# Attention phases of a two-layer kernel: a batch's value matmuls and finish steps at other places in the order

## The chip, the cores and the metric

The kernel runs on one core of one Trainium2 chip. The metric is device time in microseconds of one execution; lower is better. Three executions of the kernel before took 381.69, 383.87 and 384.30 us, median 383.87.

## The reference

The reference is two layers over 4 batches of 256 tokens of width 256: a retention block, a mixture of 8 experts, an attention block with 32 query heads over 8 key groups (head size 8), and a gated feed-forward block with 2:4 sparsity. Each block adds tanh(gate) times its result to x. The change lies in the attention block, which computes:

```
q = (Q @ w_q.T).reshape(B, S, G, HG, HD);  k, v likewise per group
scores = einsum('bnghd,bmgd->bnghm', q, k) / sqrt(HD)     # padded keys and later keys masked
attn = softmax(scores, axis=-1)
out = einsum('bnghm,bmgd->bnghd', attn, v).reshape(B, S, D) @ w_o.T + b_o
```

## The kernel before, in words

All engines have their programs written out by hand; each runs its instructions in order and waits on counted semaphores. The helper `acquire` (line 185) hands out the eight PSUM banks in rotation by kind and makes TensorE wait until the bank's last content has been read. The kind "max" has three banks (0 to 2), "exp" three (3 to 5), "turn1" and "tok1" one each (6 and 7).

The attention block runs as one phase for each of the four batches, and a phase has 24 steps (line 552 for TensorE, line 956 for ScalarE, line 1284 for VectorE). In step n of phase b the work is this.

- **Scores of the next batch** (`scores`, line 414): one matmul of 512 columns and one mask matmul into a "max" bank, four steps ahead (`LEAD`; seven ahead in phase 0). VectorE reads each bank with one maximum over keys (`row_maxima`, line 1213). After the 24th, `negate` (1218) makes the negated maxima, and `neg_turn` (432) turns them on TensorE in two transposes through the one "turn1" bank; ScalarE copies each to `nmT`, and the sync engine's queue moves them by two DMAs into `qst`. The first `weights` of the next phase waits for these DMAs through the semaphore `max_rows` (line 444).
- **Weights of this batch** (`weights`, line 439): one matmul of 512 columns into an "exp" bank. ScalarE makes the exponentials of it (line 929), and GpSimd zeroes the diagonal blocks (line 775) after exponentials 4, 8, 10 and 12 of each half.
- **Values of this batch** (`values`, line 448): four groups of 32-column matmuls, called v0 to v3 here: half 0 and half 1 of the groups, each for the first and the second 128 queries. v0 and v2 have 8 matmuls, v1 and v3 have 16. v0 and v1 are read by VectorE (`value_copy`, 1232), v2 and v3 by ScalarE (`value_turn`, 932). v0 and v1 stand at steps 20 and 22 (`VALUES_AT`). v2 and v3 stand after step 23, v2 in an "exp" bank and v3 in "tok1", each followed by two of the four leading scores of batch b+2.
- **Finish of the batch before** (`finish`, lines 462, 939, 1239): twelve steps, six for each 128 queries. Four transpose the values through "turn1" and VectorE divides by the sum (a reciprocal and a product). The fifth transposes the result through "turn1", and ScalarE copies it. The sixth projects it into "tok1", and VectorE adds it to x and makes its statistics. They stand at the odd steps 1, 3, ... 23.
- **Queries and keys of batch b+2** (phases 0 and 1 alone): two layer-norm transposes through "turn1" at steps 10 and 12, the query projection at 14, half the keys at 13 and two stack pieces at 19 and 21. After step 23 come the other half of the keys and two more stack pieces.

Phase 3 has neither scores nor queries; in their place it has four layer-norm transposes for the feed-forward block at steps 13, 15, 17 and 19.

Of the kernel before, what the change touches and what calls it, by code (L numbers as in the profile page):

```python
# [33 lines left out]

NORM_STEPS, LATE_NORM_STEPS = (13, 15, 17, 19), (3, 4, 6, 7)
KEYS_AT, STACK_AT = 13, (19, 21)
VALUES_AT = (20, 22)
NEGATE_AT, FIRST_NEGATE_AT = 22, 18
LN_EPS, GN_EPS = 1e-5, 1e-3
MASKED = -float(2.0 ** 100)  # L40
# [3 lines left out]
def build_program(nc, a, out):  # L44
# [6 lines left out]
    with ctx:  # L51
# [5 lines left out]
        def sem(name):  # L57
            if name not in sems:
                sems[name] = ctx.enter_context(nc.semaphore(name))
            return sems[name]  # L60
# [136 lines left out]
        def filled(eng, stage, i):  # L197

            eng.wait_ge(sem(stage + "_ready"), i + 1)
            return fills[stage, i]  # L200
# [4 lines left out]
        def taken(ins, stage):  # L205
            ins.then_inc(sem(stage + "_taken"), 1)
# [32 lines left out]
        def _(pe):  # L239
# [174 lines left out]
            def scores(b, n):  # L414

                s = b % 2
                q, hg, nt, quads = score_fill(n)
                if n % 12 == 0:
                    pe.wait_ge(sem(f"ks{q}_taken"), b + 1)
                    stage, i = stack_fill(b, 2 * q + 1)  # L420
                    pe.wait_ge(sem(stage + "_taken"), i + 1)
                if n == 0:
                    if b == 0:
                        loaded(pe, "caus", 2)
                dst = acquire(pe, "sa", 24 * b + n, "max").rearrange("p (j m) -> p j m", m=(nt + 1) * P)
                pe.matmul(dst, qst[:, s, q, hg, tile_cols(nt)], kblk[s][q][:, quads, 0:(nt + 1) * P],  # L426
                          start=True, stop=False, skip_group_check=True)
                diagonal = dst[:, :, nt * P:(nt + 1) * P]
                ready(pe.matmul(diagonal, identb[:, :], causb[:, 0:diagonal.shape[1], :], start=False, stop=True,  # L429
                                skip_group_check=True), "sa")  # L430
# [17 lines left out]
            def values(b, i, kind):  # L448

                q, nt = divmod(i, 2)  # L450
                stage = VALUE_STAGES[q]
                pe.wait_ge(sem("causal_done"), 8 * b + 4 * q + 2 + 2 * nt)
                dst = acquire(pe, stage, 2 * b + nt, kind)
                pe.wait_ge(sem("vp_taken"), b + 1)
                for mt in range(nt + 1):
                    for j in range(QUADS):
                        rhs = pt0[q][:, j, :, tile_cols(nt)] if mt == 0 else pt1[q][:, j, :, :]
                        ins = pe.matmul(dst[32 * j:32 * j + 32, :], vaug[:, 2 * b + mt, 4 * q + j, :], rhs,  # L458
                                        start=(mt == 0), stop=(mt == nt), skip_group_check=True)
                ready(ins, stage)  # L460

            def finish(b, n):

                nt, c = divmod(n, 6)
                i = 2 * b + nt
                if c < PER_GROUP:
                    f = 4 * i + c
                    dst = acquire(pe, "avT", f, "turn1")
                    if c == 0:
                        for stage in VALUE_STAGES:  # L470
                            pe.wait_ge(sem(stage + "_taken"), i + 1)
                    for q in range(HALVES):
                        ins = pe.transpose(dst[:, tile_cols(q)], avT[nt][:, q, c * P:(c + 1) * P], ident[:, :])  # L473
                    ready(ins, "avT")
                elif c == PER_GROUP:
                    pe.wait_ge(sem("avT_taken"), 4 * i + 4)
                    turn_pair("atT", i, att[:, i % 2, :], "turn1")
                else:
                    dst = acquire(pe, "res2", i, "tok1")[:, 0:DIM]
                    pe.wait_ge(sem("atT_taken"), i + 1)  # L480
                    for t in range(KT):
                        ins = mm(dst, actT[:, i % 2, t, :], wo1[:, t, :], t == 0, t == KT - 1)
                    ready(ins, "res2")
# [68 lines left out]
            for b in range(BATCH):  # L552
                lead = LEAD if b else FIRST_LEAD
                for n in range(24):
                    if b + 1 < BATCH and n + lead < 24:
                        scores(b + 1, n + lead)
                    weights(b, n)
                    if b >= 1 and n % 2 == 1:
                        finish(b - 1, n // 2)
                    if b + 2 < BATCH:  # L560
                        queries(b + 2, n)
                        if n == KEYS_AT:
                            keys(b + 2, "max", (0,))
                        if n in STACK_AT:
                            stack_piece(b + 2, STACK_AT.index(n), "max")
                    if b == BATCH - 1 and n in NORM_STEPS:
                        ln_turn(3, NORM_STEPS.index(n), "tok1")
                    if n in VALUES_AT:
                        values(b, VALUES_AT.index(n), "max")
                    if n == (NEGATE_AT if b else FIRST_NEGATE_AT) and b + 1 < BATCH:  # L570
                        neg_turn(b + 1, ("turn1", "turn1"))
                if b + 2 < BATCH:
                    keys(b + 2, "turn1", (1,))
                    for piece in (2, 3):
                        stack_piece(b + 2, piece, "exp")

                for i in range(2):
                    values(b, 2 + i, ("exp", "tok1")[i])
                    for n in range(i * LEAD // 2, (i + 1) * LEAD // 2):
                        if b + 2 < BATCH:  # L580
                            scores(b + 2, n)


            def half_piece(stage, w, g, j):
# [203 lines left out]
        def _(act):  # L788
# [140 lines left out]
                taken(act.activation(dst, src.rearrange("p (h n) -> p h n", n=SEQ - mt * P), ACT.Exp,  # L929
                                     bias=padcol[:, key:key + 1], scale=float(HD) ** -0.5), "sb")  # L930

            def value_turn(b):
                for nt in range(2):
                    src = filled(act, "av1", 2 * b + nt)
                    if b >= 1:
                        act.wait_ge(sem("avT_ready"), 8 * (b - 1) + 4 * nt + 4)
                    taken(act.activation(avT[nt][:, 1, :], src, ACT.Copy), "av1")

            def finish(b, n):
                nt, c = divmod(n, 6)  # L940
                i = 2 * b + nt
                if c == PER_GROUP:
                    src = filled(act, "atT", i)[:, 0:DIM]
                    if i >= 2:
                        act.wait_ge(sem("res2_ready"), i - 1)
                    taken(act.activation(actT[:, i % 2, :, :], src.rearrange("p (t n) -> p t n", t=KT), ACT.Copy), "atT")
# [9 lines left out]
            for b in range(BATCH):  # L956
                for n in range(24):
                    exponentials(b, n)
                    if b >= 1 and n % 2 == 1:
                        finish(b - 1, n // 2)  # L960
                    if b + 2 < BATCH:
                        queries(b + 2, n)
                    if b == BATCH - 1 and n in NORM_STEPS:
                        ln_turn(3, NORM_STEPS.index(n))
                    if n == (NEGATE_AT if b else FIRST_NEGATE_AT) and b + 1 < BATCH:
                        neg_turn(b + 1)
                if b + 2 < BATCH:
                    query_stack(b + 2)
                    keys(b + 2)
                value_turn(b)  # L970

            def magnitude(i):
                g, j = divmod(i, 4)
# [20 lines left out]
        def _(dve):  # L994
# [289 lines left out]
            for b in range(BATCH):  # L1284
                lead = LEAD if b else FIRST_LEAD
                if b + 1 < BATCH:
                    for n in range(lead):
                        row_maxima(b + 1, n)
                for n in range(24):
                    if b + 1 < BATCH and n + lead < 24:  # L1290
                        row_maxima(b + 1, n + lead)
                        if n + lead == 23:
                            negate(b + 1)
                    if b >= 1 and n % 2 == 1:
                        finish(b - 1, n // 2)
                    if b + 2 < BATCH:
                        queries(b + 2, n)
                        if n == KEYS_AT:
                            spread_keys(b + 2)
                        if n in STACK_AT:  # L1300
                            stack_copy(b + 2, STACK_AT.index(n))
                    if b == BATCH - 1 and n + 2 in NORM_STEPS:
                        norm(3, NORM_STEPS.index(n + 2))
                    if n in VALUES_AT:
                        value_copy(b, VALUES_AT.index(n))

            def sparsify(g, step):
# [158 lines left out]
```

## Time and profile before

| | |
|---|---|
| device time of three runs | 381.69, 383.87, 384.30 us; median 383.87 |
| span of the profiled execution | 380.5 us (its own device time is not listed) |
| TensorE, VectorE, ScalarE, GpSimd busy | 334.3, 220.0, 156.8, 100.2 us |
| the four attention phases | 176.24 to 287.24 us, 111.00 us |
| mean granted TensorE clock | 0.946; 1.00 in the four phases |

The span runs from the first to the last instruction. The device time of a run is longer by what lies around the span: 1.2 us for the shortest run and 3.8 us for the longest, if all three had this span. Busy shares over the whole span mix stages with different limits, so the attention phases are read by themselves.

### The profile page before, as it was taken

How to read it: one execution, taken by the hardware profiler on the slowest of the kernel's cores; microseconds unless marked ns; L12 is line 12 of the kernel's file. 1: busy time of each engine (PE TensorE's matmuls, PEld its weight loads, DVE VectorE, ACT ScalarE, POOL GpSimd, SP SyncE). 2: the span in 40 equal slices, each digit the busy share in tenths (PEclk: the TensorE clock that was granted, in tenths of full speed). 3: DMA queues.
4: the chain of work that ended last, by engine and by line, in shares of the span. 5: the costliest groups of instructions: out<-in, count | busy, mean ns of one | idle time of the engine just before them, and what ended most of it. 6: DMA issues, size and time to landing. Idle time of an engine off the chain costs nothing.

```text
span 380.5 us, 4562 instructions
## 1 busy us (share of the span) xinstructions
PE 334.3 (88%) x1473; PEld 201.6 (53%) x1473; DVE 220.0 (58%) x513; ACT 156.8 (41%) x327; POOL 100.2 (26%) x154
## 2 busy tenths in 40 slices
PE   3999785969999816999989999998899989999997
PEld 1485574756666404564544654643544444445885
DVE  4345976502222347889956993993342449778911
ACT  2434341333333122136867665774874233333000
POOL 7203663520000176401342334333441001000000
PEclk9999998588999756799999999999999999999999
DMA  7997000153111114500000000000000000000011
GB/s 231 364 421 210 0 15 2 65 167 101 46 53 41 55 56 166 221 0 9 0 8 2 0 0 9 0 3 8 0 2 0 2 0 0 0 1 2 28 41 41
DMA packets 14023, 22.53 MB, mean 59 GB/s; under 512 B 2049, under 2 KB 11393, under 8 KB 13186
## 3 DMA queue, kind: packets, MB, share of 16 engines
q1 hardware_dynamic: 13234, 20.16, 15.3%
q0 software_dynamic: 768, 2.10, 1.7%
q8 instruction: 12, 0.20, 0.2%
q14 instruction: 9, 0.07, 0.1%
HBM read 15.96 MB, written 6.03 MB: 58 GB/s over the span
## 4 chain that ended last, share of the span: by engine, by line
PE 65%; DVE 14%; issue 6%; POOL 5%; ACT 5%; DMA 4%; SPq 1%; ACTq 0%; DVEq 0%; POOLq 0%
PE bank L241 47%; DVE mx L1216 6%; PE bank L458 5%; PE bank L426 4%; ACT region L929 3%; PE bank L429 3%; POOL x_sorted L739 2%; PE bank L257 2%; DVE stats L999 2%; PE bank L251 2%; POOL rstd L711 1%; DVE x_sb L1039 1%; PE bank L473 1%; DMA x_sb<-in_x_dram 1%; PE bank L510 1%
## 5 line engine op out<-in xcount | busy, mean ns | idle before, releaser
L929 ACT ACTIVATE region<-bank,padcol 128x512 f32<-128x512 f32 x96 | 62.4, 695 | 18.1 <-PE bank L241 17.3
L1216 DVE TENSOR_REDUCE mx<-bank 128x2 f32<-128x512 f32 (+1 forms) x96 | 61.3, 683 | 11.7 <-PE bank L429 11.4
L241 PE MATMUL bank<-xT,e_gu 128*128 128x512 f32 x128 | 57.6, 594 | 0.5 <-ACT xT L792 0.5
L775 POOL TENSOR_SCALAR_AFFINE_SELECT region<-region 128x1024 f32<-128x1024 f32 x32 | 35.0, 1094 | 81.8 <-ACT region L929 81.7
L241 PE MATMUL bank<-qst,kblk 128*128 128x512 f32 x96 | 46.1, 490 | 0.8 <-DMA qst<-nmT 0.3
L426 PE MATMUL bank<-kblk,qst 128*128 128x512 f32 x96 | 45.1, 488 | 1.7 <-ACT qst L877 0.9
L241 PEld LDWEIGHTS bank<-xT,e_gu 128*128 128x128 f32 x128 | 23.3, 190 | 25.1 <-issue 24.3
L429 PE MATMUL bank<-causb,identb 128*128 128x256 bf16 (+1 forms) x96 | 31.8, 331 | 0.0
L241 PE MATMUL bank<-e_down,region 128*128 128x256 f32 x128 | 27.8, 379 | 0.0
L707 POOL TENSOR_SCALAR veps<-mv 128x1 f32<-128x1 f32 x40 | 11.4, 284 | 62.0 <-DVE mv L1001 59.9
L241 PEld LDWEIGHTS bank<-e_down,region 128*128 128x128 f32 x128 | 24.3, 190 | 3.7 <-issue 0.5
L1039 DVE SCALAR_TENSOR_TENSOR x_sb<-bank,tg,x_sb 128x256 f32<-128x256 f32 x24 | 11.6, 483 | 24.9 <-PE bank L241 24.8
L792 ACT ACTIVATE xT<-bank 128x256 f32<-128x256 f32 x32 | 12.3, 385 | 32.0 <-PE bank L251 31.9
L711 POOL TENSOR_TENSOR rstd<-veps,power 128x1 f32<-128x1 f32 x40 | 23.8, 595 | 3.3
L251 PE MATMUL bank<-ident,xn 128*128 128x128 f32 x48 | 12.2, 350 | 13.9 <-DVE xn L1011 11.2
L458 PE MATMUL bank<-region,vaug 128*32 128x512 f32 x192 | 23.9, 600 | 0.2
L241 PEld LDWEIGHTS bank<-qst,kblk 128*128 128x128 f32 x96 | 18.6, 196 | 9.6 <-ACT region L929 7.1
L426 PEld LDWEIGHTS bank<-kblk,qst 128*128 128x128 f32 x96 | 19.2, 200 | 8.3 <-issue 4.5
L984 ACT ACTIVATE silu<-bank 128x512 f32<-128x512 f32 x16 | 9.6, 597 | 32.5 <-PE bank L241 32.5
L1188 DVE TENSOR_TENSOR sact<-bank,silu 128x176 f32<-128x176 f32 x15 | 5.1, 342 | 30.8 <-ACT silu L895 30.8
L241 PE MATMUL bank<-e_gu,sT 128*128 x60 | 21.8, 489 | 0.5 <-ACT sT L889 0.5
L241 PE MATMUL bank<-e_down,sT 128*128 (+1 forms) x60 | 19.6, 426 | 1.4 <-ACT sT L910 1.4
(158 smaller groups left out, 543.9 us busy)
## 6 DMA issues: line engine op xcount, KB each, us to landing
e_gu<-in_e_gu_dram SPq DMA_DIRECT2D x2, 1408.0 KB, 11.9
x_sorted<-zero SPq DMA_DIRECT2D x1, 1920.0 KB, 9.1
y_sorted<-region SPq DMA_DIRECT2D x15, 128.0 KB, 1.7
x_sb<-in_x_dram SPq DMA_DIRECT2D x4, 256.0 KB, 4.2
ctxT<-in_ctxT_dram SPq DMA_DIRECT2D x2, 512.0 KB, 6.1
e_down<-in_e_down_dram SPq DMA_DIRECT2D x1, 1024.0 KB, 13.7
region<-x_sorted SPq DMA_DIRECT2D x1, 1024.0 KB, 7.3
e_gu<-in_f_gate_dram SPq DMA_DIRECT2D x1, 1024.0 KB, 4.8
```

Of the source, the lines that this page charges most:

```text
L241: return pe.matmul(dst, lhsT, rhs, start=first, stop=last)
L251: ins = pe.transpose(dst[:, tile_cols(t)], src[:, tile_cols(t)], ident[:, :])
L426: pe.matmul(dst, qst[:, s, q, hg, tile_cols(nt)], kblk[s][q][:, quads, 0:(nt + 1) * P], start=True, stop=False, skip_group_check=True)
L429: ready(pe.matmul(diagonal, identb[:, :], causb[:, 0:diagonal.shape[1], :], start=False, stop=True, skip_group_check=True), "sa")
L458: ins = pe.matmul(dst[32 * j:32 * j + 32, :], vaug[:, 2 * b + mt, 4 * q + j, :], rhs, start=(mt == 0), stop=(mt == nt), skip_group_check=True)
L707: pool.tensor_scalar(veps[:, layer, k:k + 1], mv[:, layer, k, 1:2], eps, None, ALU.add)\
L711: pool.tensor_tensor(out=rstd[:, layer, k:k + 1], in0=veps[:, layer, k:k + 1], in1=power[:, :], op=ALU.pow).then_inc(sem(f"rstd{layer}"), 1)
L775: pool.affine_select(out=block, in_=block, compare_op=ALU.is_ge, fill=0.0, base=0, pattern=[[0, 2], [0, PER_GROUP], [1, P]], channel_multi ...
L792: taken(act.activation(xT[:, :, tile_cols(tile)], src[:, 0:DIM].rearrange("p (t n) -> p t n", t=KT), ACT.Copy), f"ln{layer}")
L929: taken(act.activation(dst, src.rearrange("p (h n) -> p h n", n=SEQ - mt * P), ACT.Exp, bias=padcol[:, key:key + 1], scale=float(HD) ** -0 ...
L1039: dve.scalar_tensor_tensor(out=x_sb[:, tile, :], in0=filled(dve, stage, k)[:, 0:DIM], scalar=tg[:, g:g + 1], in1=x_sb[:, tile, :], op0=ALU ...
L1216: taken(dve.reduce_max(mx[:, b % 2, nt, quads, q, hg], src, AX), "sa")
```

## The change

v0 moves from step 20 to step 12, v1 from 22 to 20, v2 from the end of the phase to step 23, and v3 from the end of the phase to step 5 of the next phase (for the last batch it stays behind step 23). All four now take a "max" bank. ScalarE reads v2 directly after exponential 23 instead of after the stack and the keys, and v3 after exponential 5 of the next phase. The twelve finish steps stand at 2, 4, 6, 8, 10, 11 and 13, 14, 16, 17, 19, 21. The four leading scores of batch b+2 stand in one row at the end of the phase.

```
-VALUES_AT = (20, 22)
+VALUES_AT = (12, 20, 23)
+LATE_VALUES_AT = 5
+FINISH_AT = (2, 4, 6, 8, 10, 11, 13, 14, 16, 17, 19, 21)
...
                     weights(b, n)
-                    if b >= 1 and n % 2 == 1:
-                        finish(b - 1, n // 2)
+                    if b >= 1 and n in FINISH_AT:
+                        finish(b - 1, FINISH_AT.index(n))
+                    if b >= 1 and n == LATE_VALUES_AT:
+                        values(b - 1, 3, "max")
...
-                for i in range(2):
-                    values(b, 2 + i, ("exp", "tok1")[i])
-                    for n in range(i * LEAD // 2, (i + 1) * LEAD // 2):
-                        if b + 2 < BATCH:
-                            scores(b + 2, n)
+                    for n in range(LEAD):
+                        scores(b + 2, n)
+            values(BATCH - 1, 3, "max")
...
-            def value_turn(b):
-                for nt in range(2):
-                    src = filled(act, "av1", 2 * b + nt)
...
+            def value_turn(b, nt):
+
+                src = filled(act, "av1", 2 * b + nt)
...
                     exponentials(b, n)
-                    if b >= 1 and n % 2 == 1:
-                        finish(b - 1, n // 2)
+                    if b >= 1 and n in FINISH_AT:
+                        finish(b - 1, FINISH_AT.index(n))
+                    if b >= 1 and n == LATE_VALUES_AT:
+                        value_turn(b - 1, 1)
...
+                value_turn(b, 0)
                 if b + 2 < BATCH:
                     query_stack(b + 2)
                     keys(b + 2)
-                value_turn(b)
+            value_turn(BATCH - 1, 1)
...
-                    if n in VALUES_AT:
+                    if n in VALUES_AT[:2]:
                         value_copy(b, VALUES_AT.index(n))
```

VectorE's finish steps follow the same list (line 1294).

## Rows read from the trace of the kernel before

**Rows 1.** Stretches: from:to us, us; busy PE, PEld, DVE, ACT, POOL; clock; DMA
```profile
204.32:223.89 19.57, 18.93 (x97) 11.87 (x96) 18.73 (x45) 14.01 (x24) 5.47 (x5) 1.00 0.00 0
223.89:237.92 14.03, 13.46 (x89) 6.29 (x89) 7.49 (x18) 8.17 (x16) 6.20 (x9) 1.00 0.02 6
237.92:254.43 16.51, 16.39 (x84) 9.79 (x84) 15.72 (x38) 12.73 (x21) 5.47 (x5) 1.00 0.00 1
254.43:265.01 10.58, 8.89 (x62) 2.87 (x61) 4.92 (x13) 4.64 (x9) 4.81 (x7) 1.00 0.03 8
265.01:278.72 13.71, 11.46 (x54) 7.29 (x51) 5.85 (x23) 12.55 (x24) 5.47 (x5) 1.00 0.01 1
```

**Rows 2.** Timeline, end of phase 0: start, us, engine, line, op [idle before <-releaser]
```profile
199.50 1.07 PE L458 MATMUL bank<-region,vaug 128*32 128x512 f32 x8
201.27 1.29 DVE L1216 TENSOR_REDUCE mx<-bank 128x4 f32<-128x512 f32 x2 [2.94 <-PE bank L429]
201.62 1.92 PE L458 MATMUL bank<-region,vaug 128*32 128x512 f32 x16
203.48 0.50 PE L426 MATMUL bank<-kblk,qst 128*128 128x512 f32 x1
204.78 0.48 PE L241 MATMUL bank<-qst,kblk 128*128 128x512 f32 x1
205.37 0.48 PE L241 MATMUL bank<-qst,kblk 128*128 128x512 f32 x1
```

**Rows 3.** Timeline, phase 1, steps 3 to 6, VectorE and one score
```profile
207.02 1.28 DVE L1216 TENSOR_REDUCE mx<-bank 128x2 f32<-128x512 f32 x2
208.03 0.39 PE L426 MATMUL bank<-kblk,qst 128*128 128x512 f32 x1
...
208.59 1.28 DVE L1216 TENSOR_REDUCE mx<-bank 128x2 f32<-128x512 f32 x2
```

**Rows 4.** Groups by line, of the stretch 190 to 330: VectorE's value copies
```profile
L1237 DVE COPY prod<-bank 128x512 f32<-128x512 f32 x4 | 2.7, 686 | 1.9 <-PE bank L458 1.9
```

**Rows 5.** Timeline, phase 1, steps 9 and 10: users of "turn1"
```profile
211.97 0.40 PE L257 MATMUL bank<-ident,att 128*128 128x128 f32 x2
213.10 0.69 ACT L929 ACTIVATE region<-bank,padcol 128x512 f32<-128x512 f32 x1
213.18 0.44 PE L251 MATMUL bank<-ident,xn 128*128 128x128 f32 x2
```

**Rows 6.** Timeline: the turns of the maxima in phases 0 and 1
```profile
191.71 0.27 PE L437 MATMUL bank<-ident,nmx 128*64 128x128 f32 x1 [1.01 <-DVE nmx L1228]
...
229.50 0.30 PE L437 MATMUL bank<-ident,nmx 128*64 128x128 f32 x1
...
230.22 0.30 PE L437 MATMUL bank<-ident,nmx 128*64 128x128 f32 x1 [0.42 <-ACT nmT L917]
```

**Rows 7.** Chain of waits ahead of phase 0: start, us, what
```profile
173.27 0.65 SPq L687
...
173.96 2.23 DMA qst<-nmT
...
176.24 0.50 PE bank L241
```

**Rows 8.** Timeline: the same turn at the end of phase 2
```profile
260.69 0.30 PE L437 MATMUL bank<-ident,nmx 128*64 128x128 f32 x1 [0.70 <-ACT nmT L917]
...
261.32 1.08 SPq L687 DMA_DIRECT2D qst<-nmT  x2
...
265.01 0.73 PE L241 MATMUL bank<-qst,kblk 128*128 128x512 f32 x2
```

**Rows 9.** Stretch at the end of the expert stage, columns as in the first group
```profile
126.00:131.50 5.50, 4.11 (x11) 1.88 (x11) 0.51 (x3) 0.86 (x4) 0.00 (x0) 0.78 0.14 48
```

**Rows 10.** Timeline of ScalarE, phase 3
```profile
265.64 5.88 ACT L929 ACTIVATE region<-bank,padcol 128x512 f32<-128x512 f32 x10
...
283.42 0.69 ACT L929 ACTIVATE region<-bank,padcol 128x512 f32<-128x512 f32 x1 [1.21 <-PE bank L241]
```

More of the change, by code:

```diff
@@ L930, in exponentials @@
                                      bias=padcol[:, key:key + 1], scale=float(HD) ** -0.5), "sb")
-            def value_turn(b):
-                for nt in range(2):
-                    src = filled(act, "av1", 2 * b + nt)
-                    if b >= 1:
-                        act.wait_ge(sem("avT_ready"), 8 * (b - 1) + 4 * nt + 4)
-                    taken(act.activation(avT[nt][:, 1, :], src, ACT.Copy), "av1")
+            def value_turn(b, nt):
+                src = filled(act, "av1", 2 * b + nt)
+                if b >= 1:
+                    act.wait_ge(sem("avT_ready"), 8 * (b - 1) + 4 * nt + 4)
+                taken(act.activation(avT[nt][:, 1, :], src, ACT.Copy), "av1")
             def finish(b, n):
@@ L1293, in _ @@
                             negate(b + 1)
-                    if b >= 1 and n % 2 == 1:
-                        finish(b - 1, n // 2)
+                    if b >= 1 and n in FINISH_AT:
+                        finish(b - 1, FINISH_AT.index(n))
                     if b + 2 < BATCH:
```

## The prediction, made before the change was run

> **What bounds the kernel now.** I read the stretches of the attention phases first, since the change touches nothing else. Each phase falls into two parts. In the first 19 or 20 steps the scores of the next batch are made, and VectorE is full: 18.73 of 19.57 us in phase 1 and 15.72 of 16.51 in phase 2 [rows 1]. TensorE is nearly as full there, 18.93 and 16.39, though pipelined matmuls make its figure too high. In the late part no scores are left. VectorE is busy 7.49 of 14.03 us there and ScalarE 8.17, while TensorE is at 13.46: values, stack pieces and keys stand in one row on TensorE. In phase 2's late part all engines have holes (TensorE 8.89 of 10.58). In phase 3 ScalarE leads with 12.55 of 13.71. So the question for each moved instruction is whether it leaves a place where TensorE sets the pace, and what sets the pace where it arrives.
>
> The timeline at the end of phase 0 shows the late part [rows 2]. v2 (8 matmuls) starts at 199.50, v3 (16) at 201.62 and the next score at 203.48, so v3 takes 1.86 us. I take 1.0 for v0 and v2 (1.07 busy). VectorE waits 2.94 us there. In the first part the pace is VectorE's [rows 3]: two maxima and one finish step take 1.57 us (207.02 to 208.59). Of this I give 0.60 to each maximum and 0.37 to the finish step. A TensorE step without extras takes 0.59 (204.78 to 205.37 [rows 2]).
>
> **The change, phase by phase.** Times are counted in TensorE's order. A minus is a gain.
>
> *Phase 0.* v3 leaves the end: -1.86. v2 moves to step 23, which is the same row of TensorE work: 0. v0 leaves step 20: -1.0. At step 12 TensorE has room, because at step 18 it waits 1.01 us for the negated maxima [rows 6]. But VectorE's copy of v0 (0.69 [rows 4]) now comes ahead of the last four maxima and so of `negate`, and VectorE must first wait for v0's end, about 0.35 (an estimate: half a maximum and a score). I take +1.03; the bounds are 0.69, the copy alone, and 1.69, copy and all of v0. Sum -1.83. The four leading scores now stand in a row, and VectorE's reading of three "max" banks paces them; that costs nothing beyond the 5.28 us less v2 and v3 that lie between 199.50 and 204.78.
>
> *Phase 1, first part.* v3 of batch 0 stands at step 5, between weights 5 and score 10. When it starts, VectorE has two maxima and one finish step left (1.57). The next maximum can start after v3 and one score: 1.86 + 0.66 (a four-row score runs from 203.48 to a maximum at 204.25, 0.77; the shorter mask takes 0.11 off). With the score before it already counted, VectorE stands idle 1.3 us. The bounds are 0 (the spare TensorE time of 0.64 in this part [rows 1] and the later catching up hide it) and 1.86. I take +1.3, since 0.64 of room in 20 steps can't hide 1.86 at one place.
>
> Steps 10 and 12 need "turn1". Before, the transpose of a finished half stood at step 9 (211.97) and the layer-norm transpose of step 10 followed at 213.18, when ScalarE had copied it out; score and weights lay between [rows 5]. Now both stand in step 10, and exponential 10 (0.69) goes ahead of the copy. TensorE waits about 1.05 us there with nothing in between, and the score behind it arrives 1.15 later than it did relative to VectorE's other work. Bounds 0 and 1.9 (the gap of 1.21 and an exponential). VectorE also gets v0's copy and one finish step that stood in the late part: 0.65 + 0.37 = +1.02. v0 itself at step 12 lies under this. Some of VectorE's 0.84 us of idle time in this part [rows 1] vanishes: -0.38. Sum +3.09.
>
> *Phase 1, late part.* v3 -1.86, v0 -1.0. The transpose that stood at step 21 and its wait for VectorE -0.47, other waits -0.18. The turn of the maxima at step 22 loses its cover: before, v1 stood ahead of it, ScalarE had long made exponential 22, and the second transpose came 0.72 after the first (229.50, 230.22 [rows 6]). Now v1 is at step 20, and ScalarE makes exponential 22 first, with TensorE waiting: +0.67, one exponential. Sum -2.84, phase 1 +0.25.
>
> *Phase 2.* In the first part v3 of batch 1 costs +1.3, copy and finish step +1.02. Finish steps 4 and 5 now stand at 10 and 11, so the projection waits for ScalarE's copy of the transpose just issued, and finish steps 6 and 7 stand at 13 and 14 with one "turn1" bank: +0.95 together (bounds 0 and 1.9). Sum +3.27. In the late part three matmuls of weights, v1 and a projection bring the second turn of the maxima about 4.7 us after step 20. What is queued behind it matters. The sync queue issues its DMAs 0.63 later (260.69, 261.32 [rows 8]), and from issue to the first weights that use them it took 2.97 us ahead of phase 0 (173.27 to 176.24 [rows 7]). Before, a projection, v2 and v3 covered this: the next weights came 4.32 after the turn (265.01). Now one weights matmul and v2, about 1.4 us, stand there, and TensorE waits some 2.2 us. The late part becomes 4.7 + 0.63 + 2.97 = 8.3 against 10.58: -2.28. Phase 2 is +1.0.
>
> *Phase 3.* The first exponential comes 0.12 earlier after its matmul, as v3's copy no longer stands before it: -0.12. Ten exponentials take 5.88 us [rows 10], 0.577 each. Three "exp" banks let weights 5 be issued after exponential 2, 1.9 after the first starts; v3 ends at 4.07, its copy at 4.7. Exponential 6 could have started at 3.46: +1.24. The projection one step behind its transpose costs +0.4. At the end ScalarE's wait of 1.21 for v1 [rows 10] is about halved, as v0 is gone and v1 stands earlier: -0.6. Sum +0.94 with the -0.12. Behind step 23, v3 of the last batch waits for GpSimd's blanking as before: 0.
>
> The sum is -1.83 + 0.25 + 1.0 + 0.94 = +0.36 us. Against the profiled execution that is a span of 380.9 instead of 380.5. The median of the runs lies 3.4 above that span, and the same difference puts the forecast at 383.87 + 0.36, 384.2 us.
>
> **The rivals.**
>
> *TensorE's room hides the moved work (faster).* Then v3 of three batches gives 5.6 and v0 of the batches 1 to 3 gives 3.0, less 2.2 for the wait on the maxima's DMAs and 1.0 in phase 0: about -5.5, 378.4 us. For it speaks VectorE's 6.5 us of idle time in phase 1's late part, which scores could fill earlier. Against it speaks that TensorE and VectorE are both over 95% busy where the work arrives [rows 1]. Half of it, 381, is more likely than all of it.
>
> *The clock falls at the end of phase 2 (slower).* The granted clock is 1.00 in all four phases [rows 1], which is the 2.4 GHz level. At the end of the expert stage, when TensorE was busy 4.11 of 5.50 us, it fell to a mean of 0.78 [rows 9], so part of that stretch was granted 1.2 GHz. The new wait of 2.2 us lies in a late part that is already thin. It decides if the clock falls before weights 0 of phase 3. Then v3 at step 5 takes 1.86 longer, and the transposes no longer fit beside the exponentials, some 0.1 per step: +2.5 to +3.5 until the feed-forward matmuls, 387.2 us. Against it speaks that the late part of phase 2 at 84% busy kept 1.00. The Trainium skill, "TensorE: Matmul & The Clock Gate", Part 1, says that the throttled state is the default and that activity releases it. By that rule the pause speaks against this change, as it does here; no row before shows a pause of this length inside the phases.
>
> *The change moves nothing (same).* If VectorE's order paces every phase as a whole, all terms cancel and the time is 383.9. That lies in my forecast's range.
>
> **How the numbers follow.** Three runs of one kernel differ by 2.6 us, so 1% (3.8 us) is about what can be told from no change. My case, within 2.5 us of +0.36, gets 0.62, together with the cancelling. The half-hidden case (-3, 381) gets 0.14, the fully hidden one 0.09, the clock case 0.15. The bounds of the single terms add up to far more than they can reach together; half of the two widest (v3 twice, 0 to 1.86) and of the "turn1" terms gives about -2.5 and +2.5. The range 380.3 to 387.4 takes in the half-hidden case and most of the clock case. Faster by over 1%, below 380.0: all of the hidden case and a third of the half-hidden one, 0.14. Slower by over 1%, above 387.7: 0.4 of the clock case and the tail of mine, 0.12. Within: 0.74.
>
> **What would show it right or wrong.** In the profile after, phase 1's weights 0 come near 203.0 instead of 204.78. VectorE waits over 1 us once, at step 5 of phases 1 and 2. The layer-norm transpose at step 10 of phase 1 shows a wait of about 1 us. The first weights of phase 3 wait about 2 us for the DMA and start near 264.4. ScalarE waits at step 5 of phase 3. If phases 1 and 2 are each shorter by over 1 us, the room was there and the first rival holds; if the granted clock is under 1.00 between 255 and 285, the second does. The forecast is wrong if the four phases together change by more than 3 us.

## The result and the profile after

The changed kernel takes **388.36 us** (median of 4 runs, 387.32 to 389.07) against 384.09 for the kernel before (381.69 to 384.45). The ratio is 1.0123, with a 95% interval from 1.0092 to 1.0155. So it is slower, by 0.9 to 1.6%, and its median lies above the predicted range of 380.3 to 387.4. The profiled execution, the shortest of the four, has a span of 385.3 us against 380.5.

The page of the changed kernel: the span, busy times by engine, and the granted clock in 40 equal slices.

```profile
span 385.3 us, 4555 instructions
PE 335.4 (87%) x1466; PEld 203.0 (53%) x1473; DVE 219.8 (57%) x513; ACT 157.5 (41%) x327; POOL 100.5 (26%) x154
PEclk9999997589999655999999999997999999999999
```

Within the attention phases the one new mark is the 7 among the nines, in the slice from 260 to 270 us: there the clock fell. Measured from the first weights of a phase to the first weights of the next (for phase 3 to the first feed-forward matmul), the phases changed so:

| us | phase 0 | phase 1 | phase 2 | phase 3 | sum |
|---|---|---|---|---|---|
| before | 28.54 | 33.60 | 26.64 | 22.16 | 110.94 |
| after | 27.12 | 34.02 | 27.92 | 27.11 | 116.17 |
| difference | -1.42 | +0.42 | +1.28 | +4.95 | +5.23 |
| predicted | -1.83 | +0.25 | +1.0 | +0.94 | +0.36 |

The rest accounts for the span: phase 0 started 0.42 earlier in this execution, from stages that the change does not touch, and from the first feed-forward matmul to the end it is 93.33 us in place of 93.36. Three phases came out within 0.42 us of the prediction, each a little longer than predicted (0.86 together). Phase 3 missed by 4.0.

Stretches of the changed kernel that answer to [rows 1] (columns as there); they begin with weights 0 of phases 1, 2 and 3 and are about as long as there, the third is phase 2's late part:

```profile
202.94:222.50 19.56, 18.73 (x106) 11.18 (x106) 16.70 (x40) 12.68 (x22) 4.37 (x4) 1.00 0.00 1
236.97:253.50 16.53, 16.01 (x90) 8.74 (x90) 13.72 (x34) 11.25 (x18) 4.38 (x4) 1.00 0.00 1
253.50:264.88 11.38, 8.51 (x53) 4.03 (x51) 6.96 (x17) 7.15 (x13) 5.35 (x7) 0.96 0.02 7
264.88:278.60 13.72, 12.60 (x56) 6.33 (x57) 3.45 (x13) 8.91 (x16) 4.96 (x6) 0.78 0.00 0
```

VectorE, nearly full before (0.84 and 0.79 us without work), now has 2.86 us without work in phase 1's first stretch and 2.81 in phase 2's. In the last row the granted clock is 0.78; it was 1.00.

Timeline of the changed kernel, phase 1 at step 5 and at step 10 (columns as in [rows 2]):

```profile
206.88 1.92 PE L460 MATMUL bank<-region,vaug 128*32 128x512 f32 x16
208.73 0.50 PE L428 MATMUL bank<-kblk,qst 128*128 128x512 f32 x1
209.39 0.69 DVE L1221 TENSOR_REDUCE mx<-bank 128x2 f32<-128x512 f32 x1 [1.36 <-PE bank L431]
...
212.54 0.38 PE L259 MATMUL bank<-ident,att 128*128 128x128 f32 x2
213.33 0.38 ACT L948 ACTIVATE actT<-bank 128x256 f32<-128x256 f32 x1
213.76 0.44 PE L253 MATMUL bank<-ident,xn 128*128 128x128 f32 x2 [0.83 <-ACT actT L948]
214.70 0.69 DVE L1221 TENSOR_REDUCE mx<-bank 128x4 f32<-128x512 f32 x1 [0.65 <-PE bank L431]
```

Both predicted waits are there: VectorE stands 1.36 us behind v3, and the layer-norm transpose stands 0.83 us behind the copy that frees "turn1". Phase 1's weights 0 started at 202.94 (predicted 203.0), but that is luck: phase 0 was 0.41 longer than predicted and began 0.42 earlier.

Timeline of the changed kernel, end of phase 2 and start of phase 3; against [rows 8]:

```profile
260.34 0.27 PE L439 MATMUL bank<-ident,nmx 128*64 128x128 f32 x1
261.43 0.30 PE L439 MATMUL bank<-ident,nmx 128*64 128x128 f32 x1 [0.82 <-ACT nmT L919]
261.89 1.06 PE L460 MATMUL bank<-region,vaug 128*32 128x512 f32 x8
262.06 1.08 SPq L689 DMA_DIRECT2D qst<-nmT  x2
264.88 1.65 PE L243 MATMUL bank<-qst,kblk 128*128 128x512 f32 x3 [1.93 <-DMA qst<-nmT]
268.63 2.97 PE L460 MATMUL bank<-region,vaug 128*32 128x512 f32 x16
...
275.59 1.10 PE L243 MATMUL bank<-wo,actT 128*128 128x256 f32 x4 [1.02 <-ACT actT L948]
```

The wait for the DMA is 1.93 us (predicted: some 2.2). Then v3 at step 5 takes 2.97 us where the same sixteen matmuls took 1.92 in phase 1. The windows of the changed kernel say why (from:to, us; busy PE, PEld, DVE, ACT, POOL; granted clock; DMA):

```profile
263.00:264.00 1.00, 0.00 (x0) 0.00 (x0) 0.00 (x0) 0.60 (x1) 1.00 (x2) 0.99 0.16 44
264.00:265.00 1.00, 0.12 (x1) 0.12 (x1) 0.00 (x0) 0.00 (x0) 0.83 (x4) 0.50 0.07 22
268.00:269.00 1.00, 1.00 (x7) 0.40 (x9) 0.43 (x2) 0.97 (x3) 0.79 (x1) 0.50 0.00 0
270.00:271.00 1.00, 1.00 (x8) 0.20 (x4) 0.00 (x0) 0.00 (x0) 0.00 (x0) 0.60 0.00 0
271.00:272.00 1.00, 1.00 (x11) 0.39 (x4) 0.00 (x0) 0.31 (x1) 0.00 (x0) 1.00 0.00 0
```

While TensorE waits (busy 0.00), the clock goes from 1.00 to 0.50, that is from 2.4 to 1.2 GHz. It stays there until about 270.8, although TensorE is busy without a break from 265 on.

At the end of phase 3, timeline of the changed kernel:

```profile
289.26 1.92 PE L460 MATMUL bank<-region,vaug 128*32 128x512 f32 x16 [1.29 <-POOL region L777]
291.25 0.60 ACT L939 ACTIVATE amat<-bank 128x512 f32<-128x512 f32 x1 [2.61 <-PE bank L460]
291.99 1.96 PE L243 MATMUL bank<-xT,e_gu 128*128 128x512 f32 x4 [0.81 <-ACT amat L939]
```

The last v3 waits 1.29 us for GpSimd's blanking, and the feed-forward waits 0.81 for v3's copy. Before, neither wait is there: v2 and v3 ran as one row of 24 matmuls, and the first feed-forward matmul followed directly. Timeline of the kernel before:

```profile
284.17 3.07 PE L458 MATMUL bank<-region,vaug 128*32 128x512 f32 x24
287.17 1.98 PE L241 MATMUL bank<-xT,e_gu 128*128 128x512 f32 x4
```

### The profile page after: what moved, and what is told of

Its sections match the earlier page's. It is cut to its first block, busy times and chain, and to the rows that moved or that the text cites. A ratio compares the mean times of both kernels' runs of the same rounds, so it can differ in the third digit from the quotient of the medians.

```text
span 385.3 us, 4555 instructions
## 1 busy us (share of the span) xinstructions
PE 335.4 (87%) x1466; PEld 203.0 (53%) x1473; DVE 219.8 (57%) x513; ACT 157.5 (41%) x327; POOL 100.5 (26%) x154
## 4 chain that ended last, share of the span: by engine, by line
PE 66%; DVE 13%; issue 6%; DMA 5%; POOL 4%; ACT 3%; SPq 1%; another core or an unknown queue 0%; DVEq 0%; ACTq 0%; POOLq 0%
PE bank L243 49%; PE bank L460 5%; DVE mx L1221 5%; PE bank L428 4%; PE bank L431 2%; POOL x_sorted L741 2%; PE bank L259 2%; PE bank L475 2%; DVE stats L1004 2%; PE bank L253 1%; ACT region L931 1%; POOL rstd L713 1%; DVE x_sb L1044 1%; DMA qst<-nmT 1%; PE bank L512 1%
## 5 line engine op out<-in xcount | busy, mean ns | idle before, releaser
L431 PE MATMUL bank<-causb,identb 128*128 128x256 bf16 (+1 forms) x89 | 28.4, 319 | 0.0
L460 PE MATMUL bank<-region,vaug 128*32 128x512 f32 x192 | 25.0, 624 | 1.3 <-POOL region L777 1.3
```

## The experiments

Four theories, named in the expectations by letter. **C**: phase 3 pays for the fall of the clock, which comes from the pause. **Q**: phase 3 pays for the order of work in TensorE's queue (v3 at step 5, the finish steps, the last bank), whatever the clock. **S**: the order of the finish steps costs in all phases. **V**: sixteen value matmuls cost their own time where they arrive.

Lengths of phases are read from one profiled execution of each kernel. They repeat well: phase 1 took 34.02 to 34.04 us in all six executions in which its work is that of the changed kernel. The stages ahead of the phases, which no edit touches, ended anywhere from 175.8 to 178.1 us, so phases are compared here and not spans. Of each edit the lines of TensorE's program are shown; where ScalarE's order changes with them, its lines are left out.

**Keeping TensorE busy in the pause.** Eight matmuls without use fill the wait at the end of phase 2; all else is as changed.

```
+                if b == 2:
+                    stage, m = occupant[7]
+                    pe.wait_ge(sem(stage + "_taken"), m + 1)
+                    for _ in range(8):
+                        mm(banks[7][:, :], selr[:, 0:P], selr[:, 0:UNIT], True, True)
```

> The changed kernel with eight matmuls of 512 columns, whose result nobody reads, between v2 of batch 2 and the first weights of phase 3. They fill the 1.93 us for which TensorE waits for the DMAs of the maxima. Theory C (the clock): the granted clock stays at 1.00, phase 3 starts at the same place (264.9), v3 at step 5 takes 1.9 instead of 2.97, and weights 0 to v3 take 2.2 instead of 3.75: phase 3 shorter by 2.6, span 382.7 instead of 385.3, ratio to the kernel before about 1.005. Theory Q (the order of the queues in phase 3: v3 and its copy between exponentials 5 and 6, the bank of the last v3): the clock may stay up, but ScalarE waits anyway; span within 0.6 of 385.3.

Measured: 385.87 us, ratio to the kernel before 1.0077 (1.0049 to 1.0105). Phase 2 stays at 27.94, phase 3 falls from 27.11 to 25.14. Timeline and window of this kernel:

```profile
263.48 2.12 PE L243 MATMUL bank<-selr 128*128 128x512 f32 x8
265.53 0.96 PE L243 MATMUL bank<-qst,kblk 128*128 128x512 f32 x3
...
264.00:266.00 2.00, 2.00 (x9) 1.38 (x9) 0.00 (x0) 0.22 (x1) 1.83 (x5) 1.00 0.09 27
```

The filler ends when the DMA lands, so it delays nothing, and the clock stays at 1.00. The mean clock of all 7 of its runs is 0.938 or more, that of the 4 runs of the changed kernel 0.934 or less. This mean covers the whole execution, and single runs of the kernel before go down to 0.933 too, so it supports the rows and would not do alone. So the clock is part of the cause, 1.97 us in the profiled execution (theory C had expected 2.6); 2.98 of phase 3's 4.95 remain at the full clock.

**The last v3 in bank 7, as before.**

```
-            values(BATCH - 1, 3, "max")
+            values(BATCH - 1, 3, "tok1")
```

> The changed kernel, but the last v3 (batch 3) takes bank tok1 again instead of a max bank, so that the first feed-forward matmuls do not wait for ScalarE's copy of it (0.81 us in the trace). Both theories: that wait goes, span 384.5; C: the clock falls at the start of phase 3 as before. If the table load of ScalarE sets the start of the feed-forward block instead, nothing is gained and the span stays at 385.3.

Measured: 386.47 us, 1.0102 (1.0062 to 1.0142), not told apart from the changed kernel by time. The trace shows the term itself. Timeline of this kernel:

```profile
289.32 1.92 PE L460 MATMUL bank<-region,vaug 128*32 128x512 f32 x16 [1.29 <-POOL region L777]
291.18 1.98 PE L243 MATMUL bank<-xT,e_gu 128*128 128x512 f32 x4
```

The wait of 0.81 is gone, the 1.29 ahead of v3 is not. Phase 3 is 24.80, 2.31 shorter than after; of this 0.81 is the bank. The 1.50 left over is put down to the clock, which was at 0.50 for a shorter time here, from about 265.9 to 269.3 by its windows:

```profile
265.00:266.00 1.00, 0.00 (x0) 0.00 (x0) 0.00 (x0) 0.09 (x1) 0.92 (x3) 0.93 0.15 45
269.00:270.00 1.00, 1.00 (x8) 0.59 (x11) 0.36 (x3) 1.00 (x3) 0.30 (x1) 0.86 0.00 0
```

**v3 of batch 2 stays at the end of phase 2.**

```
-                    if b >= 1 and n == LATE_VALUES_AT:
+                    if 1 <= b <= 2 and n == LATE_VALUES_AT:
...
+                if b == 2:
+                    values(2, 3, "max")
```

> The changed kernel, but v3 of batch 2 alone stays at the end of phase 2 and ScalarE copies it there, as before; batches 0 and 1 keep v3 at step 5. Theory C: v3 covers the wait for the DMAs, the clock stays 1.00, and phase 3 also loses v3 at step 5; the first weights of phase 3 come 0.9 later (v3 waits for GpSimd until 263.9, ends at 265.7), phase 3 is shorter by 2.6 for the clock and 1.2 for v3; span 382.3. Theory Q alone: 0.9 later and 1.2 shorter, span 385.0.

Measured: 386.46 us, 1.009 (1.0058 to 1.0121). Phase 2 is 28.77 (+0.85), phase 3 is 23.91, at a clock of 1.00. Timeline of this kernel, the two ends of phase 3:

```profile
267.54 0.73 PE L243 MATMUL bank<-qst,kblk 128*128 128x512 f32 x2
...
291.45 1.96 PE L243 MATMUL bank<-xT,e_gu 128*128 128x512 f32 x4 [0.81 <-ACT amat L941]
```

Phase 3 is 3.20 shorter than in the changed kernel; theory Q alone had 1.2, theory C 3.8. Against the kernel with the pause filled (25.14), also at 1.00, v3 at step 5 of phase 3 costs 1.23; the prediction had 1.24.

**The turn of the maxima (both transposes) at step 20 in phase 2.**

```
-                    if n == (NEGATE_AT if b else FIRST_NEGATE_AT) and b + 1 < BATCH:
+                    if n == (FIRST_NEGATE_AT, NEGATE_AT, 20, None)[b]:
```

> The changed kernel with the turn of the maxima of batch 3 at step 20 of phase 2 instead of 22, behind v1. The DMAs then start about 1.5 us earlier. Theory C: the first weights of phase 3 come at about 263.3, the wait shrinks from 1.93 to 0.4, the clock stays 1.00; v3 stays at step 5 and still costs ScalarE 1.2. Span 385.3 - 1.6 - 2.6 = 381.1. Theory Q: only the 1.6 of the wait is gained, span 383.7.

Measured: 384.37 us, 1.0034 (1.0011 to 1.0058). Timeline of this kernel:

```profile
259.05 0.30 PE L439 MATMUL bank<-ident,nmx 128*64 128x128 f32 x1
259.77 0.30 PE L439 MATMUL bank<-ident,nmx 128*64 128x128 f32 x1 [0.42 <-ACT nmT L919]
260.40 1.08 SPq L689 DMA_DIRECT2D qst<-nmT  x2
263.27 0.96 PE L243 MATMUL bank<-qst,kblk 128*128 128x512 f32 x3 [0.64 <-DMA qst<-nmT]
```

The first weights follow the DMA's issue by 2.87 us (2.82 in the changed kernel; the prediction took 2.97), but the issue stands 1.84 us earlier in the phase, and 0.64 of wait is left. Phase 2 is 26.12, 1.80 shorter, and the clock keeps 1.00, so phase 3 is 25.15. One early turn takes away both the pause and what followed from it.

**The finish steps on odd steps, as before.**

```
-FINISH_AT = (2, 4, 6, 8, 10, 11, 13, 14, 16, 17, 19, 21)
+FINISH_AT = tuple(range(1, 24, 2))
```

> The changed kernel with the finish steps back at the odd steps 1, 3, ... 23; the values stay at their new places. Phases of the changed kernel from first weights to first weights (the last one to the first feed-forward matmul): 27.12, 34.02, 27.92, 27.11 us. Theory S (the order of the finish steps costs): two users of turn1 no longer meet in step 10 of phase 1, and the projection again stands two steps behind its transpose: phase 1 34.0 to 32.9, phase 2 27.9 to 27.4, phase 3 27.1 to 26.2; span less by 2.1 at an equal fall of the clock. Rival V (the values themselves cost it, v0 at step 12 and v3 at step 5): every phase within 0.3.

Measured: 384.36 us, 1.0031 (1.0013 to 1.0049). Phase 1 is 0.61 shorter than after, phase 2 1.09, and phase 3 (24.13) 1.01 shorter than with the pause filled, both at 1.00. Timeline of this kernel: the two users of "turn1", and the two ends:

```profile
213.99 0.38 PE L259 MATMUL bank<-ident,att 128*128 128x128 f32 x2
215.21 0.44 PE L253 MATMUL bank<-ident,xn 128*128 128x128 f32 x2
...
265.15 0.73 PE L243 MATMUL bank<-qst,kblk 128*128 128x512 f32 x2 [1.10 <-DMA qst<-nmT]
...
285.35 3.12 PE L460 MATMUL bank<-region,vaug 128*32 128x512 f32 x24
```

Score and weights lie between the users of "turn1" again, with no wait there; a projection ahead of v2 covers the blanking at the end, so v2 and v3 run as one row. Theory S holds: the order of the finish steps costs 2.7 us over the three phases. In phase 2 it does so through the turn of the maxima: with odd finish steps the DMAs are issued 1.12 us earlier in the phase, and the pause is 1.10 in place of 1.93.

**v0 back at step 20, v1 at step 22.**

```
-VALUES_AT = (12, 20, 23)
+VALUES_AT = (20, 22, 23)
```

> The changed kernel with v0 at step 20 and v1 at step 22, as before; v2, v3 and the finish steps stay at their new places. Theory S: v0's 1.0 us on TensorE goes back to the late part and VectorE's copy (0.7) leaves the early part, and v1 covers the turn of the maxima again (0.67 less): phase 0 within 0.3, phase 1 34.0 to 33.7, phase 2 within 0.3. Rival V: v0 at step 12 is what delays: phases 1 and 2 shorter by over 1 us each.

Measured: 388.31 us (386.03 to 389.57), 1.0144 (1.0106 to 1.0181). Phases 0 to 2 change by -0.35, 0.00 and +0.38: over these phases where v0 and v1 stand is neutral. Phase 3 is 25.56 at a clock of 1.00, 0.42 longer than with the pause filled. Of more use is a row that it gave by chance. In its profiled execution, the shortest of its runs, the pause is as long as in the changed kernel, and the clock does not fall (timeline, then windows):

```profile
265.23 0.96 PE L243 MATMUL bank<-qst,kblk 128*128 128x512 f32 x3 [1.92 <-DMA qst<-nmT]
...
264.00:265.00 1.00, 0.00 (x0) 0.00 (x0) 0.00 (x0) 0.00 (x0) 0.92 (x3) 1.00 0.12 35
266.00:267.00 1.00, 0.90 (x4) 0.33 (x2) 0.43 (x2) 1.00 (x3) 0.00 (x0) 1.00 0.00 0
```

**The changed kernel once more, for its clock.** No edit.

> The changed kernel as it is, once more, for the clock alone. If the fall of the granted clock at the start of phase 3 belongs to this order of work: 0.50 again from about 264 for some microseconds, phase 3 about 27.1. If it comes in some executions and not in others: a clock of 1.00 is possible there, and phase 3 would then be 25.2 with 1.9 us of wait ahead of its weights kept, near 25.6, as in the kernel with v0 late.

Measured: 387.37 us. Timeline and windows:

```profile
266.22 1.45 PE L243 MATMUL bank<-qst,kblk 128*128 128x512 f32 x3 [1.92 <-DMA qst<-nmT]
...
265.00:266.00 1.00, 0.00 (x0) 0.00 (x0) 0.00 (x0) 0.00 (x0) 0.92 (x3) 1.00 0.12 34
266.00:267.00 1.00, 0.78 (x2) 0.63 (x3) 0.00 (x0) 0.15 (x1) 0.81 (x3) 0.74 0.00 0
269.00:270.00 1.00, 1.00 (x7) 0.52 (x10) 0.43 (x2) 0.97 (x3) 0.65 (x1) 0.55 0.00 0
270.00:271.00 1.00, 1.00 (x12) 0.24 (x8) 0.00 (x0) 0.57 (x1) 0.45 (x1) 1.00 0.00 0
```

It fell again, but later and for a shorter time: a mean of 0.74 is 0.48 us at 1.00 and the rest at 0.50, so it was down from about 266.5 to 269.9, 3.4 us instead of 6.8. And phase 3 is 25.88: 0.74 over the full clock in place of 1.97. The expectation's figure of 25.6 for a kept clock was wrong as put: the wait belongs to phase 2's length, so 25.14 is what it has to be held against.

**v3 alone.** The kernel before with one part of the change: v3 of batches 0 and 1 goes to step 5 of the next phase. Finish steps, v0, v2 and all banks of the ends stay.

```
+                    if b in (1, 2) and n == 5:
+                        values(b - 1, 3, "max")
...
-                    values(b, 2 + i, ("exp", "tok1")[i])
+                    if i == 0 or b >= 2:
+                        values(b, 2 + i, ("exp", "tok1")[i])
```

> The kernel before with one part of the change alone: v3 of batches 0 and 1 at step 5 of the next phase, in a max bank. Phases of the kernel before: 28.54, 33.60, 26.64, 22.16. By the prediction's terms (-1.86 where it leaves, +1.3 where it arrives): 26.7, 33.0, 27.9, 22.2, together 109.8, ratio 0.997. If TensorE's room hides it: 26.7, 31.7, 26.6, 22.2, together 107.2, ratio 0.990. If it costs all that it gives: 26.7, 33.6, 28.5, 22.2, ratio 1.000.

Measured: 384.14 us, 1.0015 (0.9999 to 1.0032). Against before, phase 0 loses 1.77, phase 1 (one leaves, one arrives) gains 0.13, phase 2 (one arrives) gains 1.89. Timeline of this kernel, phase 2:

```profile
245.12 1.29 DVE L1221 TENSOR_REDUCE mx<-bank 128x2 f32<-128x512 f32 x2 [1.38 <-PE bank L429]
```

VectorE's wait is 1.38, but the phase pays 1.89, the whole duration of v3: none of the wait is won back later. Theory V holds in these phases: of the three sums expected, the one in which the arrival costs all that the removal gives came out within 0.13 us in every phase. The move by itself is neutral.

**All three mends together:** finish steps on odd steps, the turn at step 20 in phases 1 and 2, the last v3 in bank 7; the held-over v3 stays at step 5.

```
+FINISH_AT = tuple(range(1, 24, 2))
...
+                    if n == (FIRST_NEGATE_AT, 20, 20, None)[b]:
...
+            values(BATCH - 1, 3, "tok1")
```

> The changed kernel with three things mended: finish steps at the odd steps, the turn of the maxima at step 20 in phases 1 and 2, the last v3 in tok1. By the sums so far (theories C and S): phases 27.1, 32.4, 25.6, 23.4, together 108.5 against 110.9 of the kernel before and 116.2 of the changed one; the clock stays at 1.00; ratio to the kernel before 0.994. By rival V: 27.1, 33.5, 26.1, 24.3, together 111.0, ratio 1.000.

Measured: 382.29 us against 383.30, 0.9976 (0.9958 to 0.9994); phases 27.12, 33.33, 25.76 and 23.46, sum 109.67, which is 1.27 below before. Neither expected sum came out (108.5 by C and S, 111.0 by V): phases 2 and 3 are as C and S had them, phase 1 is as V had it. The gains do not add up: in phase 2 the early turn alone gave 1.80 and the odd finish steps alone 1.09, both together 2.16. **From this kernel two more**, each with one edit. The first puts the held-over v3 at step 11 (`LATE_VALUES_AT = 11`):

> The kernel with the finish steps on odd steps, the second turn of maxima at step 20 in phases 1 and 2 and the last v3 in another bank (phases 33.33, 25.76 and 23.46 us), and beside that the held-over v3 no longer at step 5 but at step 11 of the next phase, behind the projection of an attended block, where VectorE is busy for about 1.2 us with the residual and its statistics while TensorE waits. Theory V, the arrival of the sixteen matmuls costs their own 1.9 us wherever TensorE sets the pace: phases 1 and 2 change by less than 0.2 each, ratio to the unchanged kernel about 0.998. Rival, at step 11 TensorE has a wait that they fill: phases 1 and 2 get 0.7 shorter each, phase 3 0.3 to 0.7, and the ratio is about 0.993.

Measured: 0.998 (0.9963 to 0.9998); phases 1 to 3 are 33.49, 25.85 and 23.86, none shorter. Timeline of phase 1: the wait only moves.

```profile
215.51 1.92 PE L460 MATMUL bank<-region,vaug 128*32 128x512 f32 x16
...
218.03 0.69 DVE L1221 TENSOR_REDUCE mx<-bank 128x2 f32<-128x512 f32 x1 [1.18 <-PE bank L431]
```

The second leaves v3 of batch 2 at the end of phase 2 (the edit shown above):

> The same mended kernel, but the v3 of batch 2 stays at the end of phase 2 and does not go to step 5 of phase 3. If the arrival at step 5 costs what the removal gives: phase 2 longer by 1.2 (27.0), phase 3 shorter by 1.2 (22.2), ratio unchanged at 0.998. If phase 2's end had room for it behind the wait for the query transfer: phase 2 longer by under 0.7, phase 3 shorter by 1.2, ratio 0.996.

Measured: 381.71 us against 383.14, 0.9977 (0.996 to 0.9995). Phase 2 is 27.82 (+2.06), phase 3 21.78 (-1.68): with the pause gone, v3 costs about its 1.9 us at either place, where with the pause (28.77 against 27.92) it cost 0.85. All three mended versions are a little faster than the kernel before, by about 0.2%, less than the 1% that the prediction set as a bound.

## Why the prediction was wrong

**The step that failed** is phase 3's, "Sum +0.94", together with "as before: 0" for the last v3. Phase 3 measured +4.95. By the experiments, as far as their terms add, it is made of:

| us | predicted | measured | from |
|---|---|---|---|
| v3 at step 5 | +1.24 | +1.23 | v3 stays, against the pause filled |
| clock | 0 in the sum; a rival with 0.15 | +1.97 (+0.74 in the second execution) | the pause filled |
| order of the finish steps | +0.4 | +1.01 | finish on odd steps, against the pause filled |
| bank of the last v3 | 0 | +0.81 | the wait in the trace, gone with bank 7 |
| earlier start and shorter wait at the end | -0.72 | -0.07 | what is left to 4.95 |

The predicted terms add up to 0.92, not 0.94. The 1.29 us that the last v3 waits for GpSimd is no further term: odd finish steps take this wait away, so it lies in the 1.01.

*The clock.* The prediction named the mechanism, its place and its trigger, the wait of 2.2 us ahead of phase 3's weights 0, and took that wait into its own sum. Yet it gave the fall 0.15, because phase 2's late part had kept 1.00 at 84% busy [rows 1]. In that row all holes together are 1.69 us of 10.58, so it holds no pause of this length; the nearest row of a fall, at the end of the expert stage [rows 9], spoke the other way. The pause came out at 1.93 us, and the clock fell in three of the four profiled executions with a pause of 1.92 to 1.95 us. The Trainium skill, "TensorE: Matmul & The Clock Gate", Part 1, whose rule (the throttled state is the default, activity releases it) the prediction cited for this rival, agrees with the executions that fell; it does not tell the fourth from them, nor does any row here. The price of 2.5 to 3.5 us was too high: 1.97 and 0.74. It took v3 at step 5 as 1.86 longer; it came out 1.05 longer (2.97 in place of 1.92).

*The last v3.* Two things were overlooked there. The batch loop's end used "exp" and bank 7 ("tok1"); the diff writes "max" for both. The feed-forward's first matmuls take banks 0 to 5 in turn, so the bank of v3 is needed at once, and its copy comes into the path (0.81). And v2 at step 23 no longer has a projection ahead that covers GpSimd's blanking: v3 stands 1.29 us, which odd finish steps remove. "As before" was read off the wait that stands in both programs, not off what covers it: in the kernel before, v3 follows v2 with no idle time, in one row of 24.

**What held.** The DMA wait of 1.93 (2.2), VectorE's wait of 1.36 at step 5 (1.3) and the wait at step 10 of 0.83 (1.05). The removal of v3 was right: it gives 1.77 at the end of phase 0 (1.86). v0 at step 12, with v1 at 20, is neutral within 0.4 in each of phases 0 to 2. The starts of phase 1 at 202.94 (203.0) and of phase 3 at 264.88 (264.4) are near by luck: the phases ahead of them were 0.41 and 0.86 longer than predicted, and phase 0 began 0.42 earlier.

**Right sums from wrong terms.** In phases 1 and 2 the arrival of v3 was taken as VectorE's wait, +1.3; it is 1.89, the upper bound of the prediction. The finish order was taken at 1.15 in phase 1 and 0.95 in phase 2; undoing it gives 0.61 and 1.09. The errors cancel in phase 1. In phase 2 the turn of the maxima costs 1.80 by standing at step 22. It stood there before as well; the change took away the work that had covered its DMAs. This was the change's largest avoidable term outside phase 3.

**The rivals.** "TensorE's room hides the moved work" falls: in phases 1 and 2 an arriving v3 costs all of its time, at step 5 and at step 11. "The change moves nothing" falls by the ratio, though it is right for v3 alone and, over phases 0 to 2, for the place of v0. "The clock falls at the end of phase 2" holds as a mechanism by its own sign (a granted clock under 1.00 between 255 and 285 us), and 387.2 us was 1.2 below the median; alone it does not explain the result, since the kernel with the pause filled is still at 1.0077.

**The base of the forecast.** The prediction put the median 3.4 us above the profiled span. In every run whose span is listed the two lie 1.7 to 2.0 us apart, so the profiled execution before was one of the shorter ones. The forecast of 384.2 us does not hang on this: it is the median plus 0.36.

**What stays open**: why the clock fell in some executions with this pause and not in another, and what sets how long it stays down. From the start of the pause to the fall it was about 1.0 us in the changed kernel, 2.2 in its second execution, where TensorE had already begun again, and 1.4 with the last v3 in bank 7. What the three longer runs of the changed kernel (388.22 to 389.07 us) paid beyond the profiled one is not shown either.

## What to carry to other kernels

Where an engine was full in a stretch, work that was moved into it cost its full duration here (1.89), more than the wait that the other engine showed there (1.38). Moving it from one full stretch to another won nothing. What changed the time here was mostly what the moved work had covered: a transfer, a turn through another engine, a bank that comes free. So for each removal write down the wait that it covered, and for a new pause on TensorE put the clock into the sum with a price read from the two levels, not only beside it as a rival. When a moved operation also changes its buffer, look at who takes that buffer next.

## What the runs showed of the hardware

- The granted clock fell in a pause of 1.92 to 1.95 us, or within 0.3 us after it, in three profiled executions and kept 1.00 through one of 1.92 in a fourth; pauses of 1.10 and 0.64 us in the same place kept it, and so did every profiled execution with no pause there. Eight matmuls without use in the pause kept it as well.
- Once at 0.50, it stayed there for 6.8 us in one execution and 3.4 us in two others, with TensorE busy throughout from the end of the pause.
- At 0.50 the sixteen value matmuls took 2.97 us in place of 1.92, and the three weights matmuls of step 0 to 2 took 1.65 in place of 0.96. That is less than twice as long; of the value matmuls the last 0.8 us ran at 1.00 again, the weights matmuls lay at 0.50 throughout.
